# Adding group 0's softmax maxima with selector matmuls, and another order of the first two steps of a cross-attention block

## The reference

```python
x = layer_norm(hidden_states, ln1_w, ln1_b)
q = (x @ q_w + q_b).reshape(B, LQ, H, HD).transpose(0, 2, 1, 3)
k = (encoder_hidden_states @ k_w + k_b).reshape(B, LK, H, HD).transpose(0, 2, 1, 3)
v = (encoder_hidden_states @ v_w + v_b).reshape(B, LK, H, HD).transpose(0, 2, 1, 3)
scores = jnp.einsum('bhqd,bhkd->bhqk', q, k) * scale
scores = jnp.where(mask, scores, mask_value)
attn = jax.nn.softmax(scores, axis=-1)
out = jnp.einsum('bhqk,bhkd->bhqd', attn, v).transpose(0, 2, 1, 3).reshape(B, LQ, D)
hidden = out @ cproj_w + cproj_b + residual
y = layer_norm(hidden, ln2_w, ln2_b)
y = jax.nn.gelu(y @ fc_w + fc_b, approximate=True)
return hidden + y @ proj_w + proj_b
```

## Time and profile before

| | |
|---|---|
| median of 3 runs | 227.52 us (227.36 to 230.96) |
| profiled execution | 227.68 us |
| its span, first to last instruction | 225.9 us |
| TensorE busy (matmuls) | 212.3 us, 94% |
| VectorE busy | 175.4 us, 78% |
| ScalarE busy | 127.5 us, 56% |
| GpSimd busy | 90.2 us, 40% |
| transfers | 23.08 MB, mean 102 GB/s |

### The profile page before, as it was taken

The page is one execution under the profiler, slowest core; times in us unless marked ns, Lnnn a source line. Parts: engine busy times, 40 slices in busy tenths (PEclk is TensorE's granted clock), DMA queues, the critical chain, the costliest instruction groups (busy, mean ns, idle before and its releaser), DMA issues.

```text
span 225.9 us, 7534 instructions
## 1 busy us (share of the span) xinstructions
PE 212.3 (94%) x3126; PEld 197.8 (88%) x3126; DVE 175.4 (78%) x375; ACT 127.5 (56%) x272; POOL 90.2 (40%) x101
## 2 busy tenths in 40 slices
PE   6859997898989999999999999999999999999995
PEld 6859995697979999998999999989998999899994
DVE  3867459987999797978789797979797779778461
ACT  3557547357724894369706972589247943673240
POOL 6351506539921394109510671248312821314200
PEclk9799799999999999999999999999999999999999
DMA  6979990690000591048201870079003800100101
GB/s 196 253 251 223 241 289 21 188 192 7 0 3 1 153 237 42 3 125 245 58 4 40 217 171 4 1 230 194 3 4 96 227 12 4 52 0 3 46 0 49
DMA packets 21976, 23.08 MB, mean 102 GB/s; under 512 B 1558, under 2 KB 20662, under 8 KB 21942
## 3 DMA queue, kind: packets, MB, share of 16 engines
q1 hardware_dynamic: 21008, 21.84, 38.0%
q10 hardware_dynamic: 934, 0.75, 1.1%
HBM read 7.62 MB, written 2.10 MB: 43 GB/s over the span
## 4 chain that ended last, share of the span: by engine, by line
PE 73%; DVE 12%; issue 6%; DMA 4%; ACT 2%; POOL 2%; SPq 0%; ACTq 0%; POOLq 0%; DVEq 0%
PE bank L1104 21%; PE bank L1105 17%; PE bank L1106 17%; PE bank L1121 3%; PE scores L1134 3%; DVE recip L895 3%; PE bank L1176 3%; PE scores L1164 3%; PE bank L1183 2%; DMA w_raw_q<-in_q_w 2%; PE bank L1250 2%; DVE z L947 2%; DMA stack_kq<-n_t 2%; POOL rs L570 1%; DVE mx L850 1%
## 5 line engine op out<-in xcount | busy, mean ns | idle before, releaser
L1104 PE MATMUL bank<-proj_hi,g_hi 128*128 128x256 f32 x128 | 38.1, 298 | 1.0 <-DVE g_lo L918 1.0
L1104 PE MATMUL bank<-z_hi,fc_hi 128*128 128x256 f32 x128 | 37.6, 294 | 0.0
L1105 PE MATMUL bank<-z_hi,fc_lo 128*128 128x256 f32 x128 | 36.0, 282 | 0.0
L1105 PE MATMUL bank<-proj_hi,g_lo 128*128 128x256 f32 x128 | 36.0, 282 | 0.0
L1106 PE MATMUL bank<-z_lo,fc_hi 128*128 128x256 f32 x128 | 36.0, 281 | 0.0
L1106 PE MATMUL bank<-proj_lo,g_hi 128*128 128x256 f32 x128 | 35.9, 280 | 0.0
L570 POOL TENSOR_TENSOR rs<-ve,power 128x1 f32<-128x1 f32 x16 | 10.4, 652 | 50.8 <-DVE ve L875 50.8
L895 DVE RECIPROCAL recip<-bank 128x256 f32<-128x256 f32 x16 | 28.0, 1750 | 3.4 <-PE bank L1183 3.4
L641 ACT ACTIVATE fc_raw<-bank,fc_bias 128x256 f32<-128x256 f32 x64 | 26.6, 468 | 6.4 <-PE bank L1106 6.3
L850 DVE TENSOR_REDUCE mx<-scores 128x16 f32<-128x1024 f32 x16 | 19.5, 1220 | 10.2 <-PE scores L1134 10.2
L1104 PEld LDWEIGHTS bank<-proj_hi,g_hi 128*128 128x128 f32 x128 | 24.1, 188 | 2.7 <-DVE g_lo L918 2.1
(11 more groups left out here) (128 smaller groups left out, 565.3 us busy)
## 6 DMA issues: line engine op xcount, KB each, us to landing
stack_kq<-parts SPq DMA_DIRECT2D x48, 256.0 KB
x_in<-in_x SPq DMA_DIRECT2D x8, 256.0 KB, 3.2
ctx_in<-in_ctx_t SPq DMA_DIRECT2D x7, 256.0 KB, 3.4
out<-y SPq DMA_DIRECT2D x7, 256.0 KB, 2.1
fc_raw<-in_fc_w SPq DMA_DIRECT2D x1, 1024.0 KB, 10.0
proj_raw<-in_proj_w SPq DMA_DIRECT2D x1, 1024.0 KB, 8.8
ctx_in<-in_ctx_t ACTq DMA_DIRECT2D x1, 256.0 KB, 3.8
w_raw_k<-in_k_w ACTq DMA_DIRECT2D x1, 256.0 KB, 4.4
```

Source lines behind the costliest of these rows:

```text
L1104: mm(out_ap, a_hi, b_hi, start=first, stop=False, skip_group_check=True)
L1105: mm(out_ap, a_lo, b_hi, start=False, stop=False, skip_group_check=True)
```

## The change

Group 0's maxima no longer go through the queue. A constant `pick`, made by VectorE at the start from two slices of the identity, selects for a head the two rows of `n_t` that hold its maximum; `shift_first` adds them with a second matmul into the same place. `n_t` now has 128 partitions instead of 16 (of the groups behind, the queue still takes the first 16). The SP list gets a wait: stacks of the next group are sent only when the second `n_t` of the group before has landed; x and ctx are loaded two groups ahead, behind the stacks, and y is stored one step later. In the first step w_q is loaded ahead of the columns, q's column sums stand behind `make_k`, group 1's `normal1` stands ahead of `left_q`. In the second step fc's column sums stand in two halves of 16 matmuls, behind `weigh(b, 0)` and behind group 2's first `make_v`; fc's high part and rest are made for each k with its own semaphore count; the rest of proj is made by GpSimd in four quarters, and TensorE waits for them one by one; many items change place, and the `keep_clock` counts change.

The core of the diff:

```diff
+        pick = sb("pick", [P, H // KC, S], BF16)
-        n_t = [sb(f"n_t{p}", [N_PARTS * H // KC, KC * P], BF16) for p in range(TT)]
+        n_t = [sb(f"n_t{p}", [P, KC * P], BF16) for p in range(TT)]
...
             # sync, second_step: behind the load of proj_b
+                load_x(Group(0, 3))
+                load_ctx(Group(0, 3))
...
             # sync
             def full_step(a, b, c, ahead=True):
-                if ahead:
-                    load_x(Group(a.j, a.c + 1))
-                    load_ctx(Group(a.j, a.c + 1))
+                sp.wait_ge(n_stacked[1], b.count(16))
+                if c.c:
+                    store(Group(0, c.c - 1))
                 sp.wait_ge(shifted, a.count(4, -4))
                 stack_mask(a)
                 stack_parts(a)
-                store(c)
+                if a.c + 2 < G:
+                    load_x(Group(a.j, a.c + 2))
+                    load_ctx(Group(a.j, a.c + 2))
...
             # gpsimd
+            def rest_of_proj(m):
+                gp.tensor_tensor(proj_lo[:, 2 * m:2 * m + 2, :], proj_raw[:, 2 * m:2 * m + 2, :],
+                                 proj_hi[:, 2 * m:2 * m + 2, :].bitcast(F32), ALU.subtract).then_inc(w_split["proj"], 1)
             def second_step(a, b):
+                rest_of_ctx(Group(0, 2))
                 third_k(a)
                 third_q(a)
-                rest_of_ctx(Group(0, 2))
+                pool.wait_ge(n_split, 2)
                 rest_of_w("c")
-                pool.wait_ge(bias_ready, 3)
+                pool.wait_ge(bias_ready, 2)
                 x_and_bias(b)
+                rest_of_o(b, 0)
                 third_k(Group(0, 2))
-                third_q(Group(0, 2))
-                rest_of_o(b, 0)
                 rest_of_o(b, 1)
                 row_scale(b, 0)
                 row_scale(b, 1)
+                third_q(Group(0, 2))
+                pool.wait_ge(z2_made, 2)
                 x_and_bias(a)
                 pool.wait_ge(w_high["proj"], 1)
-                gp.tensor_tensor(proj_lo[:], proj_raw[:], proj_hi[:].bitcast(F32),
-                                 ALU.subtract).then_inc(w_split["proj"], 1)
+                rest_of_proj(0)
+                rest_of_proj(1)
             # full_step, first one: behind it
+                    rest_of_proj(2)
+                    scale_1(Group(0, 3))
+                    rest_of_o(b, 0)
+                    rest_of_proj(3)
...
             # scalar, second_step
                 lead_k(a)
+                high_of_ctx(Group(0, 2))
                 lead_q(a)
                 second_k(a)
                 second_q(a)
-                high_of_ctx(Group(0, 2))
-                act.wait_ge(w_loaded["fc"], 16)
-                scaled_high("fc", fc_hi, fc_raw, "ln2_w")
+                high_of_fc(0)
+                high_of_z(Group(0, 2))
                 keep_maxima(b, 0)
-                stack_maxima(b, 0)
-                keep_v(a, zeroed=True)
-                high_of_z(Group(0, 2))
-                keep_maxima(b, 1)
-                stack_maxima(b, 1)
                 act.wait_ge(w_loaded["c"], 16)
                 high(w_hi["c"], w_raw["c"], w_high["c"])
+                high_of_fc(1)
+                exp(b, 0)
+                keep_maxima(b, 1)
                 lead_k(Group(0, 2))
-                exp(b, 0)
                 lead_q(Group(0, 2))
                 exp(b, 1)
+                keep_v(a, zeroed=True)
+                o_lead(b, 0)
                 second_k(Group(0, 2))
-                second_q(Group(0, 2))
-                o_lead(b, 0)
                 keep_maxima(a, 0)
                 stack_maxima(a, 0)
+                second_q(Group(0, 2))
                 o_lead(b, 1)
...
             # vector
+                ve.tensor_tensor(pick[:], ident_b[:, 0:heads].unsqueeze(2).broadcast_to([P, heads, S]),
+                                 ident_b[:, heads:2 * heads].unsqueeze(2).broadcast_to([P, heads, S]),
+                                 ALU.add).then_inc(pick_ready, 1)
             # first_step
                 left_k(a)
+                normal1(Group(0, 1))
                 left_q(a)
-                normal1(Group(0, 1))
             # second_step
                 normal1(Group(0, 2))
+                maxima(b, 0)
+                rest_of_z(Group(0, 2))
+                maxima(b, 1)
+                rest_of_fc(0)
+                rest_of_fc(1)
                 dve.wait_ge(bias_summed, 2)
-                ...
-                maxima(b, 0)
-                maxima(b, 1)
-                rest_of_z(Group(0, 2))
...
                 variance2(b, 0)
+                dve.wait_ge(bias_summed, 3)
+                ve.tensor_tensor(fc_bias[:], bank4[:, 1, 0:MB], col[:, COLS["fc_b"]:COLS["fc_b"] + MB],
+                                 ALU.add).then_inc(bias_ready, 1)
                 maxima(a, 1)
...
             # tensor
+            def shift_first(g, p):
+                q, k = q_stack[g.slot], k_stack[g.slot]
+                pe.wait_ge(pick_ready, 1)
+                pe.wait_ge(n_kept, g.count(2, p + 1))
...
+                                mm(out_at, k[0:SCORE_ROWS, h % 8, p, h // 8, rows],
+                                   q[0:SCORE_ROWS, h % 8, p, h // 8, rows],
+                                   start=True, stop=False, skip_group_check=True)
+                                last = mm(out_at, pick[:, h % 8, :], n_t[p][:, first:first + S],
+                                          start=False, stop=True, skip_group_check=True)
             # first_step
-                keep_clock(scores[:, 0, 0:P], 38)
-                pe.wait_ge(col_loaded, 16)
-                pe.wait_ge(w_loaded["q"], 16)
-                column_sums(bank7[:, 0, 0, 0:KC], w_raw["q"], "ln1_b", range(KC)).then_inc(bias_summed, 1)
+                keep_clock(scores[:, 0, 0:P], 48)
                 turn_z(a)
                 keep_clock(scores[:, 0, 0:P], 4)
                 pe.wait_ge(w_split["k"], 1)
                 make_k(a)
+                pe.wait_ge(col_loaded, 16)
+                pe.wait_ge(w_loaded["q"], 16)
+                column_sums(bank7[:, 0, 0, 0:KC], w_raw["q"], "ln1_b", range(KC)).then_inc(bias_summed, 1)
             # second_step
+                keep_clock(scores[:, 0, 0:P], 12)
                 turn_z(a)
+                keep_clock(scores[:, 0, 0:P], 12)
                 make_k(a)
                 make_q(a)
-                pe.wait_ge(w_loaded["fc"], 16)
-                pe.wait_ge(bias_ready, 1)
-                column_sums(bank7[:, 1, 0, 0:MB], fc_raw, "ln2_b", range(MB)).then_inc(bias_summed, 1)
...
                 score(b, 1)
+                make_q(Group(0, 2))
+                turn_maxima(b, 1)
+                shift_first(b, 0)
...
+                shift_first(b, 1)
...
                 weigh(b, 0)
+                pe.wait_ge(w_loaded["fc"], 16)
+                pe.wait_ge(n_kept, 2)
+                sums_of_fc(range(MB // 2))
                 pe.wait_ge(stacks_set[1], 16)
                 first_score(a)
-                keep_clock(bank5[:, 0, 0:P], 10)
                 weigh(b, 1)
+                pe.wait_ge(w_split["c"], 1)
+                pe.wait_ge(q_left, 2)
+                project(b, 0, a)
+                turn_maxima(a, 0)
+                score(a, 1)
+                pe.wait_ge(v_kept, 2)
                 make_v(Group(0, 2), 0)
+                pe.wait_ge(n_kept, 3)
+                sums_of_fc(range(MB // 2, MB)).then_inc(bias_summed, 1)
+                project(b, 1, a)
                 make_v(Group(0, 2), 1)
+                keep_clock(bank1[:, 0, 0:P], 4)
+                pe.wait_ge(bias_ready, 3)
+                turn_maxima(a, 1)
             # full_step, first one
-                    keep_clock(bank1[:, 0, 0:P], 24)
+                    keep_clock(bank7[:, 0, 0, :], 14)
...
+                    keep_clock(bank7[:, 0, 0, :], 8)
                 shift(b, 1)
```

91 lines of the change are left out of this document (55 added, 36 removed).

## The result

The changed kernel takes 227.2 us (median of 20 executions, 224.59 to 231.47) where the kernel before, timed beside it, takes 229.25 (20, 227.36 to 231.98): ratio 0.988 [0.9849, 0.9912], the brackets being the 95% interval. Medians are of all executions, while ratios leave out the slow ones, more than 1.5% above the fastest of their kernel. By the medians the change gains 2.05 us, by the ratio about 1.2%, 2.8 us, and not the 7.7 us forecast; 219.8 and the range 217.5 to 223.6 are both missed. The gain is clear of 1.0 and still under the 2% that the prediction took as the least that counts. The profiled execution took 227.06, its span is 225.3.

A forecast was written before the change was run, and what follows sets the result against it. TensorE bounds the kernel from 65.4 to 200 us, so only the filling ahead can shrink: 7.0 to the mark, 0.4 from proj's quarters and 0.3 in the steady steps make 7.7 us, giving 219.8 us, range 217.5 to 223.6.

The forecast's parts named there:

- Which part of the kernel matters: TensorE is busy from 65.4 to 200 us, so the change can only win ahead of 65.4.
- Part 1: First step: normal1 ahead of left_q gives group 1's z at 13.9 instead of 16.96; turned 2.9 us earlier.
- Part 2: Group 0's stack sets the next mark: first score at 22.0 instead of 27.02, bounds 21.5 and 23.1.
- Rival (a): Group 0's stack lands at 23.1 to 24 because the last copies hang on q_second: 221 to 222 us; chance 0.15.
- Part 3: Group 0's maxima without the queue, selector matmuls 0.65 per half: first reciprocal at 32.8 instead of 39.94, 7.1 us.
- Rival (b): Half-clock stretches around fc's sums cost up to 1.6 us each, one hidden behind VectorE; 222 to 224 us; chance 0.12.
- Part 4: First reciprocal to the mark: VectorE's list the same, 12.2 us against 12.1; turn_z2 at 45.2, mark at 58.0.
- The collision on normal2: End of VectorE's list before turn_z2: group 2's third_q (1.20) replaces xb beside the second normal2 (1.36).
- proj's quarters: Before the mark: proj's rest in four pieces of 1.15 us gives back 0.4, bounds 0 and 1.3.
- Part 5: Steady steps: SP's wait for n_t's landing takes traffic off one late landing; gain 0.3 us, bounds 0 and 0.4.
- rival (c): SP's wait makes the steady steps' stacks late, TensorE idles before scores: 228 us and up; chance 0.05.
- Rival (d): The new order makes a new wait that takes back the queue's gain; 3 to 4 us stay, 224; chance 0.08.

The follow-up runs named there:

- b_again: The kernel before, run again with no edit for a second profile: 231.33 us, ratio 1.01 to the kernel before.
- b_normal_first: The kernel before with one thing moved, VectorE's normal1 of group 1 ahead of left_q of group 0: 229.74 us, ratio 0.9984.
- after: The changed kernel's first run and profile, against the kernel before: 227.2 us, ratio 0.988.
- a_again: The changed kernel run again with no edit, for a second profile: 227.21 us, ratio 0.9934 to the kernel before.
- after_fourth: The changed kernel run a fourth time with no edit: 226.42 us, ratio 0.986 to the kernel before.
- a_no_sp_wait: The changed kernel without SyncE's wait for n_t's landing at the head of each steady step: 226.38 us, ratio 0.9734 to the kernel before.

## Why the prediction was wrong

- **Which part of the kernel matters** was right: the steady steps did not move, the gain lies ahead of 67 us.
- **Part 1** was right that normal1 escapes third_k: z takes 0.74 at 13.61, in the 13.1 to 13.85 forecast, and also 0.73 to 0.74 in the other three profiles, but at 14.23 to 14.94. The rest of its gain was the profile's: turn_z is at 7.3 to 7.9 in the four (7.35 forecast, 7.69 before), and the half clock from 8.5 to 12.0 is missing in all other profiles of the old first step too. Group 1's z is turned at 14.40 to 15.73, which against b_again's 15.37 is little. That part 1 is worth nothing until the stack is earlier had been said; b_normal_first shows it.
- **Part 2 failed**, 2.7 us. "The copies start into the idle stretch", so 22.0, was taken from the first copy. The last copy left SyncE at 18.36 instead of 18.18, and the first score came at 24.66, 25.27, 24.85 and 24.99. Nor do only the last two copies hang on q's second part: four of the six stand behind it and take 2.6 us to issue. It was to be there at 15.3, and was at 15.8 in after, at 16.4 to 17.1 in the other three, and at 13.8 in b_again. Part 1's own edit delays it, by 0.6 in b_normal_first. Rival (a) named q_second and priced it at 1.1 to 2, still too little: I had reasoned a landing at 23.1 out of w_c's, which no row showed, since TensorE never waited for the stack before.
- **Part 3** was right in mechanism and in one profile of four in size (10.4 in a_again, 10.8 forecast). shift_first's halves took 1.1 us, fc_lo 3.49 beside w_lo_c's 2.25. Missing was the supply of instructions: up to 2.43 us in TensorE. I costed instructions by their busy time alone, 0.65 per half for the 64 selector matmuls. In after, the miss of 2.0 is the clock instead: with 6.9 us at 0.51 the way from the first to the second score took 4.84 us, in a_again 2.75. Rival (b) had one such stretch hidden behind VectorE; this one was on the path, which now ran through TensorE.
- **Part 4 failed**, 1.9 us: the list of VectorE "is the same", but what stands between was not followed. Three waits of VectorE make it up: 0.26 for group 1's score, behind the first half of the sums; 0.71 more on n_wide, over which the moved third_k now lies; 1.04 for the second half of the sums, part of it at half clock. Together 2.0, the whole difference of 14.27 to the 12.27 of the kernel before. In after_fourth, with no half clock, they are 0.26, 0.71 and 0.28, and 13.50 is 12.27 and 1.25. The collision on normal2, 1.24 at 50.38, was forecast. The Trainium skill, page SBUF — State Buffer, section "SBUF: two separate sides", has a VectorE instruction in a two-port mode and GpSimd exclude each other; the trace agrees (0.17 alone, 0.88 beside third_k), and I had applied it to z and not to this small instruction, whose cost all of VectorE's list behind it shares.
- **proj's quarters** gave about what was said: turn_z2 to the part at L1143 12.71 instead of 13.23 before, that is 0.5. But 0.4 came back, as o_lo of group 1 comes at 65.44 behind the last quarter and ctx_lo, and project waits (second score 2.83 after the part, 2.44 before). Net 0.1.
- **Part 5** had 0.3, measured 0.0. The wait for n_t did go, but one of 0.22 for a stack came, in the other three profiles 0.40 to 0.74 in one or two steps: that is rival (c)'s sign, TensorE idle in the steady steps before a score, at a small part of its price. a_no_sp_wait has neither.

Summed up for the profiled execution: 2.7 + 2.0 + 1.9 + 0.3 (turn_z2 to the second score, 15.54 where 15.67 less 0.4 was forecast) + 0.3 (steady) = 7.2, which is up to rounding its span less the forecast's, 225.3 less 218.2. What came true of the 7.7 there is 0.6; at equal clock over the pooled executions it is 1.8 to 2.4. Rival (d), new waits of 3 to 4 us by the new order, comes nearest to what happened; I gave it 0.08, because I had looked at the new order for each edit and not along the whole list.

## What to carry to other kernels

Before forecasting from a profile, take a second one of the same kernel: here the first score came at 27.02 in one and at 29.09 in the other. When an edit is to bring work forward, find the last of the transfers or parts it waits for, not the first, and treat a wait that no row shows as unpriced. After reordering, walk every engine's list once more beside GpSimd's and write down what now overlaps, the tiny instructions too. Where many small matmuls follow each other, count instructions as well as busy time: 64 more of them with a busy time of 1.0 us cost about 4 us, and 64 put where the engine waits anyway brought no stop.

## What the runs showed that I had not expected

- TensorE stopped for 0.88 to 2.46 us among small matmuls, each time until 1.24 to 1.63 us behind a 16 KB packet of the instruction queue; of four profiles of the changed kernel two have such a stop.
- The stretches at half clock fall at other places in each profile of an identical kernel: 23.5 to 30.4 and 40.6 to 44.0 in after, 38.5 to 41.9 and 45.3 to 48.7 in a_again, none in after_fourth. From a mean clock of 0.99 to 0.985 and to 0.977 the changed kernel's span grows by 0.6 and 0.7 us.
- Taking load off the queues moved the stack's end little: 24.66 to 25.27 with fc_w ahead of it, 23.39 with fc_w behind.
